# Own half of x kept in SBUF with eight load slots for the other half, and an even order of matmuls inside each attention head

## The reference, cut to what matters

```python
xn = layernorm(x)                             # x: (4, 2048, 4096)
# attention with low-rank q and k, v; 32 heads
C_q  = xn @ Wq_d + bq_d                       # rank 12
C_kv = xn @ Wkv_d + bkv_d                     # rank 4
q = (C_q @ W_qk + b_qk).reshape(b, s, 32, 4)
attn = softmax(einsum('bqhd,bkd->bhqk', q, C_kv) / 2)
V = (C_kv @ Wv_u + bv_u).reshape(b, s, 32, 128)
s = einsum('bhqk,bkhd->bqhd', attn, V).reshape(b, s, 4096) @ Wo + bo
# base product with a routed low-rank part, 28 experts of rank 8, top 2
base = xn @ base_W.T
lora = einsum over the two chosen experts of (xn @ lora_A.T) * gate @ lora_B
g = silu(base + lora)
out = x + s * g
```

## Time and profile before

| | us |
|---|---|
| median of the runs shown (2 runs) | 2205.57 (2193.84 and 2217.3) |
| profiled execution | 2106.59 |
| its span, slowest core (core 1) | 2105.1 |
| spans of the eight cores | 2044.1 to 2105.1 |
| TensorE busy / VectorE / ScalarE / POOL, share of the span | 88% / 18% / 33% / 15% |

### The profile page before, as it was taken

The page is one execution under the profiler, slowest core; times in us unless marked ns, Lnnn a source line. Parts: engine busy times, 40 slices in busy tenths (PEclk is TensorE's granted clock), DMA queues, the critical chain, the costliest instruction groups (busy, mean ns, idle before and its releaser), DMA issues.

```text
span 2105.1 us, 20135 instructions; the slowest of 8 cores (2044.1 to 2105.1 us)
## 1 busy us (share of the span) xinstructions
PE 1850.1 (88%) x7186; PEld 618.0 (29%) x7186; DVE 386.6 (18%) x482; ACT 691.4 (33%) x680; POOL 312.0 (15%) x409
## 2 busy tenths in 40 slices
PE   3587439999999999999999999999998699999998
PEld 0122013222222222222222222222222244444443
DVE  0055031112112111111121111111111111111111
ACT  2301405444444443343444343444334000000000
POOL 4212210100101100010001000010000222222221
PEclk7677559999999997777999778899778799999999
DMA  9969742332422422223224222242220799999996
GB/s 101 123 85 142 111 40 26 32 44 25 50 26 25 50 26 25 26 30 40 31 26 50 26 25 26 26 50 26 26 26 10 96 178 166 170 166 175 179 169 141
DMA packets 318021, 148.08 MB, mean 70 GB/s; under 512 B 290932, under 2 KB 291076, under 8 KB 317700
## 3 DMA queue, kind: packets, MB, share of 16 engines
q0 software_dynamic: 303776, 104.78, 45.7%
q1 hardware_dynamic: 14152, 42.03, 5.5%
HBM read 217.97 MB, written 25.17 MB: 116 GB/s over the span
## 4 chain that ended last, share of the span: by engine, by line
PE 75%; DVE 11%; DMA 8%; issue 4%; ACT 2%; POOL 1%; DVEq 1%; ACTq 0%; POOLq 0%; SPq 0%
PE arena L846 30%; PE arena L1044 21%; PE arena L871 13%; PE arena L706 8%; DMA xst<-xT_own 4%; DMA xst<-xT_oth 2%; DVE qb L914 2%; DVE aoT L776 2%; DVE dinvb L770 2%; DVE a2b L907 2%; ACT xsq L634 1%; DVE xnT L376 1%; DMA bw_bf<-bwt 1%; PE arena L225 0%; DMA wo_bf<-wo 0%
## 5 line engine op out<-in xcount | busy, mean ns | idle before, releaser
L974 ACT ACTIVATE pbuf<-arena 128x1024 bf16<-128x1024 f32 x512 | 519.6, 1023 | 728.7 <-PE arena L871 726.8
L846 PE MATMUL arena<-xnT,bw_bf 128*128 128x512 bf16 x2048 | 601.9, 451 | 15.2 <-DMA bw_bf<-bwt 15.2
L1044 PE MATMUL arena<-aoT,wo_bf 128*128 128x512 bf16 x2048 | 445.1, 381 | 15.9 <-DMA wo_bf<-wo 15.9
L871 PE MATMUL arena<-qb,ckv_b 4*128 4x512 bf16 x1024 | 335.6, 400 | 34.0 <-DVE qb L914 13.3
L706 PE MATMUL arena<-pbuf,kaug 128*8 128x512 bf16 x1024 | 286.0, 393 | 48.2 <-DVE a2b L907 47.9
L846 PEld LDWEIGHTS arena<-xnT,bw_bf 128*128 128x128 bf16 x2048 | 208.2, 111 | 370.1 <-issue 238.5
L722 POOL DMA_DIRECT2D bw_bf<-bwt x128 | 112.5, 899 | 1155.2 <-PE arena L871 1038.9
L1044 PEld LDWEIGHTS arena<-aoT,wo_bf 128*128 128x128 bf16 x2048 | 200.7, 98 | 260.7 <-issue 22.1
L1058 ACT ACTIVATE g_f<-gsl 128x1024 f32<-128x1024 f16 x32 | 33.8, 1057 | 412.8 <-DVE ost L1072 412.8
L1026 POOL DMA_DIRECT2D wo_bf<-wo x128 | 112.2, 897 | 334.7 <-PE arena L1044 322.3
L871 PEld LDWEIGHTS arena<-qb,ckv_b 4*128 4x128 bf16 x1024 | 66.4, 93 | 294.3 <-issue 292.9
(11 more groups left out here) (128 smaller groups left out, 593.8 us busy)
## 6 DMA issues: line engine op xcount, KB each, us to landing
bw_bf<-bwt POOLq DMA_DIRECT2D x128, 256.0 KB, 6.0
wo_bf<-wo POOLq DMA_DIRECT2D x128, 256.0 KB, 8.7
xst<-xT_own POOLq DMA_DIRECT2D x64, 256.0 KB, 6.0
g_f<-xT_own SPq DMA_DIRECT2D x32, 512.0 KB, 7.0
outT<-ost SPq DMA_DIRECT2D x32, 512.0 KB, 4.2
xst<-xT_oth POOLq DMA_DIRECT2D x32, 256.0 KB, 5.4
gscr<-fsb POOLq DMA_DIRECT2D x32, 256.0 KB, 6.8
gsl<-gscr SPq DMA_DIRECT2D x32, 256.0 KB, 4.6
```

Source lines behind the costliest of these rows:

```text
L846: mm = t.matmul(arena[0:128, FC + c0:FC + c0 + cw], lhsT, rhs, start=st_, stop=sp_, skip_group_check=True)
L871: mm = t.matmul(arena[0:128, PB[p] + c0:PB[p] + c0 + cw], ckv_b[0:KL, kt * 128:(kt + 1) * 128], qbs[h % 2][0:KL, c0:c0 + cw], start=True, ...
L974: inst = s.activation(pbuf[:, sl * T:(sl + 1) * T], arena[0:128, spair[(h, kt)]:spair[(h, kt)] + T], AF.Exp)
L1044: mm = t.matmul(arena[0:128, PW + c0:PW + c0 + cw], wo_bf[:, (mo % 2) * D + ki * 128:(mo % 2) * D + (ki + 1) * 128], aoT[:, ki * T + c0:ki ...
```

## The change

- `xst` has eight slots in place of four. In the statistics of the own half the tiles are loaded straight into their place in `xnT`. A load waits only for the landing of the load four before it. ScalarE and TensorE read x there.
- Pass b has no loads: VectorE works in place on `xnT`, after the statistics' matmul and Square of that tile.
- The loads of the other half use all of `xst`. Its first four wait for the landing of the last four own tiles, the later ones for the load four before and for matmul and Square of the tile eight before. The small loads of L413 to L420 follow the own tiles directly on POOL's queue.
- In a head the base matmuls are spread over kt 0 to 13 (five each, four at the last two), and each kt has one `a2block`, that of the key tile three before. The three last key tiles of a head are taken at kt 0, 1 and 2 of the next.

```diff
-        xst = sbw(es1, "xst", [128, 4 * T], BF16)
+        xst = sbw(es1, "xst", [128, 8 * T], BF16)
...
-                I(g.dma_start(out=xst[:, kt * T:(kt + 1) * T],
+                I(g.dma_start(out=xnT[:, kt * T:(kt + 1) * T],
...
+            own = bk == "so"
             for kt in range(KT):
-                sl = kt % 4
-                if not (bk == "so" and kt < 4):
+                sl = kt % 8
+                buf = xnT if own else xst
+                off = (kt if own else sl) * T
+                if not (own and kt < 4):
                     @block.gpsimd
-                    def _(g, kt=kt, sl=sl):
-                        W(g, *slot_ev.get(sl, ()))
-                        I(g.dma_start(out=xst[:, sl * T:(sl + 1) * T],
+                    def _(g, kt=kt, sl=sl, buf=buf, off=off):
+                        if own:
+                            W(g, (bk, "x", kt - 4))
+                        elif kt < 4:
+                            W(g, ("so", "x", KT - 4 + kt))
+                        else:
+                            W(g, (bk, "x", kt - 4), (bk, "sT", kt - 8),
+                              (bk, "sq", kt - 8))
+                        I(g.dma_start(out=buf[:, off:off + T],
                                       in_=dsrc.ap()[kt * 128:(kt + 1) * 128, :]),
-                          "dX%d" % sl, (bk, "x", kt), n=16)
+                          "dX%d" % (kt % 4), (bk, "x", kt), n=16)
...
         for kt in range(KT):
-            sl = kt % 4
-
-            @block.gpsimd
-            def _(g, kt=kt, sl=sl):
-                W(g, *slot_ev.get(sl, ()))
-                I(g.dma_start(out=xst[:, sl * T:(sl + 1) * T],
-                              in_=dx.ap()[kt * 128:(kt + 1) * 128, :]),
-                  "dX%d" % sl, ("b", "x", kt), n=16)
-            slot_ev[sl] = (("b", "xn", kt),)
-
             @block.vector
-            def _(v, kt=kt, sl=sl):
+            def _(v, kt=kt):
                 vself(v)
-                W(v, ("b", "x", kt), ("so", "meanc"))
+                W(v, ("so", "meanc"), ("so", "sT", kt), ("so", "sq", kt))
                 I(v.scalar_tensor_tensor(xnT[:, kt * T:(kt + 1) * T],
-                                         xst[:, sl * T:(sl + 1) * T], 1.0,
+                                         xnT[:, kt * T:(kt + 1) * T], 1.0,
                                          mrs_f[:, :], ALU.mult, ALU.subtract),
                   "sV", ("b", "xn", kt))
...
                 for kt in range(SKT):
-                    if kt % 2 == 0 and kt <= SKT - 4:
-                        evens_left = (SKT - 4 - kt) // 2 + 1
-                        emit_ffn(-(-(len(fq) - fpos[0]) // evens_left))
-                    if kt % 2 == 1:
-                        for g_ in (kt - 4, kt - 3):
-                            if g_ < 0:
-                                if h > 0:
-                                    a2block(t, h - 1, SKT + g_)
-                            else:
-                                a2block(t, h, g_)
+                    if kt < SKT - 2:
+                        emit_ffn(-(-(len(fq) - fpos[0]) // (SKT - 2 - kt)))
+                    if kt < 3:
+                        if h > 0:
+                            a2block(t, h - 1, SKT - 3 + kt)
+                    else:
+                        a2block(t, h, kt - 3)
```

More of the change, by code:

```diff
@@ L203, in stats_pass, with _ @@
         def stats_pass(bk, dsrc, ca, cbk, r2, first, extra=None, inject=None):
+            own = bk == "so"
             for kt in range(KT):
-                sl = kt % 4
-                if not (bk == "so" and kt < 4):
+                sl = kt % 8
+                buf = xnT if own else xst
+                off = (kt if own else sl) * T
+                if not (own and kt < 4):
                     @block.gpsimd
-                    def _(g, kt=kt, sl=sl):
-                        W(g, *slot_ev.get(sl, ()))
-                        I(g.dma_start(out=xst[:, sl * T:(sl + 1) * T],
+                    def _(g, kt=kt, sl=sl, buf=buf, off=off):
[7 more added lines that the diff above has]
+                        I(g.dma_start(out=buf[:, off:off + T],
                                       in_=dsrc.ap()[kt * 128:(kt + 1) * 128, :]),
-                          "dX%d" % sl, (bk, "x", kt), n=16)
+                          "dX%d" % (kt % 4), (bk, "x", kt), n=16)
                         if inject and kt in inject:
                             inject[kt](g)
-                slot_ev[sl] = ((bk, "sT", kt), (bk, "sq", kt))
                 @block.tensor
-                def _(t, kt=kt, sl=sl):
+                def _(t, kt=kt, buf=buf, off=off):
                     W(t, (bk, "x", kt), (bk, "sq", kt))
@@ L222, in _ @@
                     if extra is not None:
-                        extra(t, kt, sl)
+                        extra(t, kt, off)
                     for c0, cw in CH:
                         t.matmul(arena[0:8, ca + c0:ca + c0 + cw], ones8[:, :],
-                                 xst[:, sl * T + c0:sl * T + c0 + cw],
+                                 buf[:, off + c0:off + c0 + cw],
                                  start=(kt == 0), stop=(kt == KT - 1),
@@ L475, in _, with ckv_oth_extra @@
                               ALU.subtract), "sV", ("gdel",))
-        def ckv_oth_extra(t, kt, sl):
+        def ckv_oth_extra(t, kt, off):
             for c0, cw in CH:
@@ L480, in ckv_oth_extra @@
                          wkv_b[:, kt * KL:(kt + 1) * KL],
-                         xst[:, sl * T + c0:sl * T + c0 + cw],
+                         xst[:, off + c0:off + c0 + cw],
                          start=(kt == 0), stop=False, skip_group_check=True)
@@ L627, in _ @@
                 for kt in range(KT):
-                    sl = kt % 4
+                    src_ = (xnT[:, kt * T:(kt + 1) * T] if bk == "so"
+                            else xst[:, (kt % 8) * T:(kt % 8 + 1) * T])
                     war = (bk, "sT", kt - 2)
@@ L634, in _ @@
                     Ip(s.activation(xsq[:, (kt % 2) * T:(kt % 2 + 1) * T],
-                                    xst[:, sl * T:(sl + 1) * T], AF.Square),
+                                    src_, AF.Square),
                        "sS", (bk, "sq", kt))
```

## The result

| us | before | changed |
|---|---|---|
| median of the runs | 2157.59 (2105.02 to 2232.45, 10 runs) | 1880.57 (1874.54 to 1971.12, 11 runs) |
| profiled execution | 2106.59 | 1880.33 |
| spans of the eight cores | 2044.1 to 2105.1 | 1861.3 to 1878.1 |

The ratio is 0.884, with a 95% interval of 0.880 to 0.889: 11 to 12% faster. The forecast was 1880, and the time lies in its range.

What follows compares the result with a forecast made beforehand. Bound by TensorE, full in the heads (63% of the span) but losing clock behind lean stretches. Core 1: 290.3 + 1103 + 24.3 + 454.5 = 1872, 1874 with 1.5 around it; forecast 1880 us, range 1850 to 1985 (about 0.8).

Steps and rivals of the forecast that it cites:

- Price of a head: Heads at 2.4 GHz: 138 matmuls at 0.216 us plus 47 changes of kind at about 0.10, taken as 34.3 us.
- The five waits: TensorE's waits in the heads (two a2b, qb, dinvb, aoT), 81.8 us over all heads, should all vanish.
- rival D: In the heads, waits or a dearer change of kind stay: 60 to 90 us, 1935 to 1965 us; chance 0.15.
- The clock: TensorE in heads 1 to 31 keeps 2.4 GHz, since lean stretches inside a head and the waits at its end go.
- A: Rival: the clock in the heads goes on falling whatever the order; 2025 us profiled, 2124 as a run; chance 0.10.
- B: Rival: short runs keep the heads' clock down, 64.1 us a low head, about 2,820 us if all; chance 0.03.
- C: Rival: the heads' mean clock settles between, about 0.83, so no change, 2,105 to 2,205 us; chance 0.04.
- Head 0: The first head enters at 1.2 GHz, low for about 12 us: 40 us, bounds 36 and 64.
- Pass b: Dropping its loads and working in place gains 0, as loads and VectorE were already hidden under TensorE.
- Statistics of own x: Loads straight into xnT, no longer waiting for Square and matmul, gain 5 us; bounds 0 and 6.
- Statistics of the other half: Its first eight loads run under pass b, 24 tiles remain: 51 us instead of 66, gain 15, bounds 10 and 22.
- the two readings: Median 99 us above the profiled run: more low-clock heads (1874, twice as likely) or evenly slower by 1.047 (1962).

Runs made afterwards that it cites:

- bursts_nowait: Kernel before with q, bcd, up one key tile earlier, a head's last three a2blocks at kt 1 of the next, its first at kt 3: 1845.47 us, ratio 0.861.
- wait_back: Changed kernel with a head's last a2block moved from kt 2 to kt 3, directly before the new head's first: 2031.3 us, ratio 0.940.
- best: Changed kernel's loads joined with the head order of bursts_nowait (runs of ten base matmuls): 1825.17 us, ratio 0.847.
- four_slots: Changed kernel, but a load of the other half waits for matmul and Square of the tile four before instead of eight: 1896.27 us.
- bursts_odd: Kernel before with q, bcd and up at kt 5, 7, 9 instead of 6, 8, 10; runs of ten and a2b waits stay: 1930.39 us, ratio 0.900.

## Why the prediction was right, and where it wasn't

**Price of a head: right.** 138 x 0.216 + 47 x 0.10 = 34.5 was the sum and 34.5 was measured; the 34.3 that I took for a change "a little under 0.10" was 0.2 too low, 6 us over the heads. The unshown change from 128 to 8 columns costs 0.10, the value of the nearer row.

**The five waits: right.** 0.5 us is left of 81.8, and ScalarE's exp at kt 14 and 15, my candidate for rival D, makes TensorE wait for 0.3 us once.

**The clock: right in the result, too simple in the reason.** All heads together hold 0.99, the single one shown 1.00, and A, B and C are out as forecasts of this kernel. But the prediction gave the even order as much credit as the missing waits ("those inside the head are gone"). The runs show that the old bursts hold the clock just as well without their waits (bursts_nowait), and that in the even order the clock falls too once one wait is put back (wait_back). The prediction had also misread what stands before a fall. It names the end of a head, "three kt without L846, then the two a2b waits"; but between those three kt and the waits stand the twenty L846 of kt 0 and 2. Of the 58 falls on core 1 of before between 330 and 1626 us, every one begins within 2.5 us of a wait of TensorE, 27 behind a2b and 31 behind qb, dinvb or aoT, and none behind the three kt without L846 and without a wait. Rival B had a true core: with short runs the clock came back late once it had fallen, or at the start.

**Head 0: 40 us predicted.** From 280.7 to 1395, less 31 x 34.5, leaves 44.8 on core 1, and 38.8 on core 7. One window of core 1 of the changed kernel; then the first row of the heads of best, core 1; then a window from the start of its heads on core 2, its slowest:

```profile
280.70:305.00 24.30, 24.30 (x54) 0.50 0.35 32
```
```profile
279.43 4.07 PE L845 MATMUL arena<-xnT,bw_bf 128*128 128x512 bf16 x10 [12.80 <-DMA bw_bf<-bwt]
```
```profile
287.30:312.00 24.70, 24.70 (x56) 0.50 0.36 32
```

With the even order the low clock lasts 26 us on two cores and 13 on the other six. With runs of ten it lasted 3 to 6 us on six cores of best; there the first ten L845 take less than the 4.38 of ten wholly at the low clock. But on cores 2 and 7 it lasted 26 us in spite of runs of ten and of a TensorE without idle time. So runs of ten help at the start of head 0 without ensuring anything, and what decides there isn't shown.

**Pass b: right.** No load, 60.4 us instead of 60.9.

**Statistics of own x: mis-sized.** Predicted 5, bounds 0 and 6; measured 10.7 on core 1 (last L231 at 99.49, last L239 at 88.78) and 9.6 on the median core. The step that failed is that I priced one stretch only, from 70 to 97 us, and took the rest to be at the rate of the DMA. From 1.5 to 40 us the kernel before moved this:

```profile
1.50:40.00 38.50, 15.00 (x38) 0.75 1.10 90
```

90 GB/s against 108 after (3.47 and 4.14 MB). The 0.67 MB between them are 4.7 us at the 143 GB/s of the next 30 us, and with the 5.7 of the stretch that I did price they make 10.4. In that stretch POOL of before waited 22.2 us for Square and matmuls; after, it waited 17.6 us there, all of it for landings.

**Statistics of the other half: right in size, half right in reason.** Predicted 15, measured 17.6 on core 1 (66.2 to 48.6 from the transposes to the last key product) and 14.7 on the median core (62.1 to 47.4 from the first to the last key product). I had put it down to eight tiles fetched early; but four were early before, and four_slots shows no gain on the median core from the place of the loads under pass b. It was the depth; on core 1 some 3 us were the first tile, which came late before.

**The sum.** 280.7 + 1114.3 + 25 + 454.7 = 1874.7 on core 1, against 290.3 + 1103 + 24.3 + 454.5 = 1872. Ten too much for the front and eleven too little for the heads cancelled each other, so the sum is better than its terms. The forecast of 1880 is 6 us above it, added for the other reading of the median; that the median met it within 1 us is luck.

**The median.** The first of the two readings held: the median run of the changed kernel (1880.57) is its profiled execution (1880.33), and the factor of 1.047 is gone from the median, though one run of the changed kernel still took 1971.12. The 99 us to explain were in part the choice of runs: the two known then were among the longer ones, and the median of ten is 2157.59. How much of the 99 us was heads at the low clock can't be told, since those two runs have no trace.

## What to carry to other kernels

On an engine that is 95% busy, waits of a microsecond can cost several times their length, because TensorE's clock falls behind them; so read the granted clock by stage, find in the timeline what stands before each fall, and take away the waits there first: moving the q, bcd and up products by one key tile gave a ratio of 0.900, where the whole change has 0.884. Where a producer is late, look for a place in the order that has long matmul runs behind it before reordering the whole loop, and keep runs of ten rather than five, which cost fewer changes of kind (1.6 us a head) and, after the falls inside the heads here, had the clock back sooner. And price a transfer stage over its whole length, by its bytes, not by its leanest window.

## What the runs showed of the hardware

- A change between weights of different shape costs 0.10 us at full clock in each pair of a key tile: 128*128 to 128*8, 128*8 to 4*128 and 4*128 to 128*128. It isn't so for every pair: two matmuls of 4*128 followed by one of 1*128 took 0.44 us (L867 to L748, 686.45 to 686.89 on core 7 of the changed kernel), which is without a price.
- After a fall inside a head the clock was back in some 3 us with ten base matmuls in a row (bursts_odd), and in about 10 us in most falls with runs of five among narrower matmuls (wait_back). At the start of head 0 it took 13 or 26 us with runs of five, and mostly 3 to 6 us with runs of ten, but 26 on two cores of best.
- Three kinds of wait of 0.3 to 0.7 us each, 34 us in all, carried most of the loss: without them alone the kernel is 10% faster.
- 3.9 us of matmuls with few rows or columns of weights, without a base matmul and without a wait, were followed by no fall in 31 heads; the same time with 1.54 us of waits in it by one at 11 of 31 turns.
- A wait of 0.26 us in a gap of 5.0 us between base matmuls was enough for falls, at 32 of 62 such waits.
